# The first stage of a four-part network rewritten: heads as 32-row and 32-column tiles of the array, six unrolled slots, weights rounded by ACT

## The reference

```python
x = x + attn_a(layernorm(x), Wq, Wk, Wv, Wo, norm_w)      # this case's stage
x = x + ffn(layernorm(x), Wqkv, ..., W2, b2)              # 6 layers
x = x + attn_b(layernorm(x), W_Q, W_K, W_V)
x = x + ffn(layernorm(x), Wqkv, ..., W2, b2)              # the same 6 layers again

def attn_a(h):                                            # 8 heads of 16, chunks of 64
    q, k, v = h @ Wq.T, h @ Wk.T, h @ Wv.T
    o = causal linear attention: state (sum of k v^T of earlier chunks) times q,
        plus (q k^T * lower triangle) v inside the chunk
    z = cumsum(k, over tokens)
    o = o / max(|sum_over_the_head(q * z)|, 1)
    o = o * rsqrt(mean_over_the_head(o * o) + 1e-5) * norm_w
    return o @ Wo.T
```

## Time and profile before

| | |
|---|---|
| median of 3 runs | 3269.31 us (3267.53 to 3271.12) |
| the profiled execution's own time | 3269.6 us |
| its span, first to last instruction | 3267.8 us |
| mean granted clock of TensorE | 0.976 of 2.4 GHz |
| PE / DVE / ACT / POOL busy | 94% / 90% / 69% / 56% of the span |

### The profile page before, as it was taken

One profiled execution on the slowest core, in us unless ns is written; L12 is line 12 of the kernel. 1 busy time (PEld: TensorE's weight loads), 2 busy tenths in 40 slices (PEclk: granted clock), 3 DMA queues, 4 the chain that ended last, 5 costly groups with the idle time before them and its releaser, 6 DMA issues.

```text
span 3267.8 us, 93879 instructions
## 1 busy us (share of the span) xinstructions
PE 3067.1 (94%) x37848; PEld 1899.2 (58%) x37848; DVE 2927.5 (90%) x2712; ACT 2266.0 (69%) x3691; POOL 1814.5 (56%) x822
## 2 busy tenths in 40 slices
PE   5768999999999999999999999999999999999997
PEld 3535665565565565566566655665665655655663
DVE  4549999999999999999999999999999999999995
ACT  1136777777777777777666777777777777777774
POOL 5525555555555555555454555655655655656651
PEclk8778999999999999999999999999999999999998
DMA  5534454454454454455344445445445445445442
GB/s 174 185 99 113 105 147 118 105 147 118 104 146 119 104 145 121 103 144 141 87 120 107 104 105 145 121 103 145 120 103 146 119 105 146 117 106 146 115 117 57
DMA packets 254252, 398.01 MB, mean 122 GB/s; under 512 B 51132, under 2 KB 84984, under 8 KB 254136
## 3 DMA queue, kind: packets, MB, share of 16 engines
q1 hardware_dynamic: 254136, 396.48, 46.4%
HBM read 64.71 MB, written 19.92 MB: 26 GB/s over the span
## 4 chain that ended last, share of the span: by engine, by line
PE 39%; DVE 23%; ACT 19%; issue 9%; POOL 1%; SPq 1%; DMA 1%; DVEq 0%; ACTq 0%; POOLq 0%
PE ps L783 6%; PE ps L741 5%; PE ps L801 5%; PE ps L817 5%; PE ps L762 5%; PE ps L722 4%; DVE f_mx L1297 4%; ACT f_ab L1029 3%; DVE f_p L1300 3%; ACT f_u L1028 3%; DVE f_p L1312 3%; ACT ps L1040 3%; PE ps L724 3%; PE ps L723 3%; ACT f_p L1046 3%
## 5 line engine op out<-in xcount | busy, mean ns | idle before, releaser
L1226 POOL TENSOR_TENSOR f_w<-f_w,f_ab 128x1024 f32<-128x1024 f32 x192 | 549.0, 2859 | 527.3 <-DVE f_w L1277 527.3
L1231 POOL TENSOR_TENSOR f_ab<-f_w,f_rn 128x1024 f32<-128x1024 f32 x192 | 594.3, 3095 | 390.9 <-DVE f_rn L1287 374.1
L1222 POOL TENSOR_TENSOR f_u<-f_u 128x512 f32<-128x512 f32 x384 | 588.6, 1548 | 363.3 <-ACT f_u L1028 363.2
L1029 ACT ACTIVATE f_ab<-ps,f_pa 128x512 f32<-128x512 f32 x768 | 542.0, 706 | 1.2
L1028 ACT ACTIVATE f_u<-ps 128x512 f32<-128x512 f32 x768 | 467.0, 608 | 96.7 <-PE ps L724 91.5
L1277 DVE TENSOR_TENSOR f_w<-f_ab,f_tan 128x1024 f32<-128x1024 f32 x384 | 500.9, 1345 | 4.3 <-POOL f_ab L1231 2.3
L783 PEld LDWEIGHTS ps<-f_tb,f_v 128*64 128x64 f32 x6144 | 396.4, 138 | 102.7 <-issue 86.5
L783 PE MATMUL ps<-f_tb,f_v 128*64 128x160 f32 (+1 forms) x6144 | 442.7, 297 | 12.2 <-DMA f_tb<-f_pt 9.9
L1040 ACT ACTIVATE ps<-ps 128x512 f32<-128x512 f32 x384 | 204.7, 574 | 340.4 <-PE ps L741 340.1
L722 PE MATMUL ps<-f_xh,f_wh 128*128 128x512 f32 x768 | 380.7, 496 | 53.2 <-ACT f_ab L1029 43.7
L741 PE MATMUL ps<-f_u,f_ones 128*128 128x512 f32 x768 | 368.8, 601 | 6.1 <-POOL f_u L1222 5.1
(11 more groups left out here) (170 smaller groups left out, 4975.6 us busy)
## 6 DMA issues: line engine op xcount, KB each, us to landing
f_kb<-f_ab SPq DMA_DIRECT2D x384, 256.0 KB, 3.6
f_qb<-f_ab SPq DMA_DIRECT2D x384, 256.0 KB, 3.6
f_tb<-f_pt SPq DMA_DIRECT2D x1344, 64.0 KB
f_wh<-split_w SPq DMA_DIRECT2D x48, 384.0 KB, 4.4
f_wl<-split_w SPq DMA_DIRECT2D x48, 384.0 KB, 4.2
a_w_raw<-wqkv SPq DMA_DIRECT2D x24, 384.0 KB, 4.1
split_w<-a_w_hi SPq DMA_DIRECT2D x24, 384.0 KB, 2.3
split_w<-a_w_lo SPq DMA_DIRECT2D x24, 384.0 KB, 2.8
```

What stands on the lines that cost most here:

```text
L1029: nc.scalar.activation(ab[:, g % 2, i, :], bank("qk", g, i), ACT.Identity, scale=pa[:, g, i:i + 1]).then_inc(qk_read.sem, 1)
L1222: nc.gpsimd.tensor_tensor(u[:, 2 * i + 1, :], u[:, 2 * i, :], u[:, 2 * i + 1, :], ALU.add).then_inc(sq_sum[i].sem, 1)
L1226: nc.gpsimd.tensor_tensor(w[:, 0:2, :], w[:, 0:2, :], ab[:, k % 2, 0:2, :], ALU.add).then_inc(q_sum.sem, 1)
L1231: nc.gpsimd.tensor_tensor(ab[:, k % 2, 0:2, :], w[:, 0:2, :], rn[:, 0:1, :].broadcast_to([128, 2, N]), ALU.mult).then_inc(rope_q.sem, 1)
```

## The change

The function is the same, the data flow of `stage_a` is new, and `stage_ffn` is as it was.

- Heads are taken in pairs of one 32-row strip. q is copied twice (even and odd heads of each strip, `qm`), k once, v twice into arrays with zeros at the other parity (`vz`), all by ACT. Scores: for each tile of tokens four products of 32 rows and 256 columns, one for each strip of rows, into four banks (`tile_position=(32 * p, 0)`). Values: for each tile eight products of 128 rows, 32 columns of weights and 128 tokens (`tile_position=(0, 32 * p)`), so that the result comes out with the feature on the partition, and no transpose is left. DVE masks 2048 columns at a time, twice a batch.
- The division by the denominator and the norm are one expression: `o * (ss + 1e-5 * max(d, 1)^2)^-0.5`, by sums over the head as a product with `blockmask`.
- Six slots written out instead of a loop; slot k holds the front f of batch k, the middle s of batch k-1 and the end e of batch k-2, interleaved on each engine.
- The weight halves: ACT makes the rounded one, four copies of 128 x 768 a slot between its own operations (`round_weights`), POOL subtracts; four buffers; SP loads quad n+4 ahead of the stores of quad n.
- Loads: PE waits for x of its batch and the mean matrix only, ACT and later PE for 8 tables; x comes in four pieces, each with its semaphore.

The core of the new code (waits left out where they name only the operation before; functions of one instruction left out where the text says what they do):

```diff
+                SLOTS = [tuple(b if 0 <= b < B else None for b in (k, k - 1, k - 2)) for k in range(B + 2)]
...
+                    sp.dma_start(xT[:, cols(0)], x_rows[:, cols(0)]).then_inc(x_in[0], 16)
+                    sp.dma_start(mean_w[:, :], tabs["mean_w"]).then_inc(x_in[0], 16)
+                    for dst, src in ((wq, wa["wq"]), (wk, wa["wk"]), (wv_wk, wa["wv_wk"]), (parity, tabs["parity"]), (causal, tabs["causal"]),
+                                     (blockmask, tabs["blockmask"]), (wo, wa["wo"]), (nw, wa["nw"])):
+                        sp.dma_start(dst[:, :], src).then_inc(tables, 16)
...
+                    for n in range(QUAD_W):
+                        sp.wait_ge(lo_done, n + 1)
+                        if n + NW < QUAD_W:
+                            load_raw(n + NW)
+                        for part, w in enumerate((w_hi, w_lo)):
+                            sp.dma_start(split_w[n, part], w[:, n % NW].bitcast(F32)).then_inc(split_out[n % NW], 16)
...
+                    for n in range(QUAD_W):
+                        if n >= NW:
+                            pool.wait_ge(split_out[n % NW], 32 * (n // NW))
+                        pool.wait_ge(hi_done, n + 1)
+                        nc.gpsimd.tensor_tensor(w_lo[:, n % NW], w_raw[:, n % NW], w_hi[:, n % NW].bitcast(F32), ALU.subtract).then_inc(lo_done, 1)
...
+                    def scores(b, part):
...
+                        for i in (2 * part, 2 * part + 1):
+                            for p in range(4):
+                                rows = slice(32 * p, 32 * p + 32)
+                                last = nc.tensor.matmul(ps[:, p, 256 * (i % 2):256 * (i % 2) + 256], ks[rows, tile(i)], qm[rows, :, tile(i)], start=True, stop=True,
+                                                        tile_position=(32 * p, 0))
...
+                    def values(b, part):
...
+                        for i in (2 * part, 2 * part + 1):
+                            if i:
+                                for a in range(2):
+                                    nc.tensor.matmul(ps[:, O, tile(i)], state[:, i - 1, :], qm[:, a, tile(i)], start=a == 0, stop=False, skip_group_check=True)
+                            for a in range(2):
+                                for p in range(4):
+                                    rows = slice(32 * p, 32 * p + 32)
+                                    last = nc.tensor.matmul(ps[rows, O, tile(i)], vz[:, i, a, rows], st[:, part, p, 2 * (i % 2) + a, :], start=i == 0 and a == 0, stop=a == 1,
+                                                            skip_group_check=True, tile_position=(0, 32 * p))
...
+                    def round_weights():
+                        n = next(quads)
+                        act.wait_ge(raw_in[n % NW], 16 * (n // NW + 1))
+                        if n >= NW:
+                            act.wait_ge(split_out[n % NW], 32 * (n // NW))
+                        nc.scalar.activation(w_hi[:, n % NW], w_raw[:, n % NW], ACT.Copy).then_inc(hi_done, 1)
```

More of the change, by code:

```diff
@@ L114, in _, with tile @@
+                def tile(i):
+                    return slice(128 * i, 128 * i + 128)
+                SLOTS = [tuple(b if 0 <= b < B else None for b in (k, k - 1, k - 2)) for k in range(B + 2)]
                 @block.sync
                 def _(sp):
[L116 to L133, removed]
@@ L137, in _ @@
+                    for j in range(NW):
+                        sp.wait_ge(split_out[j], 32 * (QUAD_W // NW))
                 @block.gpsimd
                 def _(pool):
[L139 to L149, removed]
+                    nc.gpsimd.memset(vz[:, :, :, :], 0.0).then_inc(cleared, 1)
@@ new lines, in mean2, with variance2 @@
+                    def mean2(b):
+                        pe.wait_ge(A["x1"], b + 1)
+                        nc.tensor.matmul(ps[:, Y, :], mean_w[:, :], xT[:, cols(b)], start=True, stop=True).then_inc(A["mean2"], 1)
+                    def variance2(b):
+                        pe.wait_ge(A["sq2"], b + 1)
+                        nc.tensor.matmul(ps[:, Y, :], mean_w[:, :], sq2[:, :], start=True, stop=True).then_inc(A["var2"], 1)
+                    for f, s, e in SLOTS:
+                        if f is not None:
+                            mean(f)
+                        if s is not None:
+                            scores(s, 0)
+                        if e is not None:
+                            project_out(e)
+                        if s is not None:
+                            states(s)
+                        if f is not None:
+                            variance(f)
+                        if s is not None:
+                            scores(s, 1)
+                            values(s, 0)
+                        if e is not None:
+                            mean2(e)
+                        if s is not None:
+                            denominator(s)
+                            values(s, 1)
+                        if e is not None:
+                            variance2(e)
+                        if f is not None:
+                            project(f)
+                        if s is not None:
+                            squares(s)
@@ L278, in _, with square, deviation @@
-                    act.preload_act_table_set("natural_log_exp_and_others")
-                    act.wait_ge(loaded, 16 * LOADS)
-                    steps_of(act, step)
+                    def square(b):
+                        act.wait_ge(A["xc"], b + 1)
+                        nc.scalar.activation(sq[:, :], xc[:, :], ACT.Square).then_inc(A["sq"], 1)
+                    def deviation(b):
+                        act.wait_ge(A["var"], b + 1)
+                        nc.scalar.activation(sq[:, :], ps[:, M, :], ACT.Ln, bias=EPS).then_inc(A["lnv"], 1)
+                        act.wait_ge(A["lnv"], b + 1)
+                        nc.scalar.activation(ps[:, M, :], sq[:, :], ACT.Exp, scale=-0.5).then_inc(A["rstd"], 1)
@@ new lines, in _ @@
+                    act.wait_ge(tables, 16 * N_TABLES)
+                    for f, s, e in SLOTS:
+                        if f is not None:
+                            square(f)
+                            deviation(f)
+                        round_weights()
+                        if e is not None:
+                            square2(e)
+                        if s is not None:
+                            denominator(s)
+                        round_weights()
+                        if e is not None:
+                            deviation2(e)
+                        if s is not None:
+                            squares(s)
+                        round_weights()
+                        if f is not None:
+                            keys_and_queries(f)
+                            values(f)
+                            values_by_parity(f)
+                        round_weights()
+                        if s is not None:
+                            norm(s)
```

390 lines of the change are left out of this document (179 added, 211 removed).

## The result

| | before | after |
|---|---|---|
| median | 3266.46 us (6 runs, 3261.76 to 3271.12) | 3282.02 us (6 runs, 3279.39 to 3292.10) |
| ratio | | 1.0054 [1.0042, 1.0066] |
| first stage, to the first load of `zT` | 207.59 us | 116.60 us |
| the rest of the span | 3060.21 us | 3164.10 us |

The account below looks back on a forecast made before the run. The prediction took the first stage as a chain with PE in most links, no engine full; slots at two thirds high clock plus the tail end it at 132 instead of 206.3 us, gain 74.3, total 3195, range 3177 to 3230.

Parts of the forecast that it names:

- the 206.25 us: The changed first stage's length before, out of 3267.8 us; forecast to end at 132, a gain of 74.3.
- The tripwire on a second stage changed by more than 5 us: Sign of a wrong forecast: the second stage, expected to last 3061.5 us as before, changing by over 5 us.
- The start: First slot: the last table lands at 7.4 us, so ACT starts its square then instead of at 11.69.
- two thirds high: PE's clock in a full slot: high two thirds of the time, giving 25 us a slot.
- rival 1: First stage: PE's clock high throughout, stage 114 us, gain 92, total 3177; chance 17%.
- the tail of 7.3: End of the first stage: quads 22 and 23 behind deviation2 make it end 17.8 us after `scale` instead of 10.5.
- rival 3: First stage: weight loads set the pace, stage 170 us, gain 36, total 3233; chance 6%.
- the contention that I costed at nothing: DVE in a full slot: contention over SBUF costed at nothing, with a bound of 1 us a slot.
- the sum: PE's work in a full slot with four tiles at once: 16.0 us high clock, scores and values 1.7 each.
- rival 5: Score products: strips load weights one after another, 8 us more, 3203; inside the forecast's 55%.
- rival 4: Score and value tiles don't overlap: 3296 with the clock low, 3213 with it high; chance 3%.
- the way in and out of a group: Change of tiling on PE: 0.18 us an excursion, six of them 1.1 us a slot.

Follow-up runs that it names:

- 109: The kernel before with 109 more PE instructions (waits already met) at the end of PE's first-stage list: 3322.77 us.
- 125: The kernel before with 125 more PE instructions (waits already met) in the first stage: 3384.26 us.
- 141: The kernel before with 141 more PE instructions (waits already met) in the first stage: 3276.43 us.
- 200: The changed kernel with 200 more PE instructions (waits already met) at the end of PE's first-stage list: 3189.91 us.
- 236: The changed kernel with 236 more PE instructions (waits already met) at the end of PE's first-stage list: 3224.03 us.
- 100: The changed kernel with 100 more PE instructions (waits already met) at the end of PE's first-stage list: 3214.62 us.
- quads_ahead: The changed kernel with 40 added PE instructions and ACT's 24 weight roundings placed earlier, none in the last slot: 3169.26 us, ratio 0.9698 to the kernel before.
- pool_rounds: The changed kernel with 40 added PE instructions, POOL making the rounded weight half again and ACT none: 3162.21 us, ratio 0.968 to the kernel before.
- the 40: 40 more PE instructions (waits already met) ending PE's first-stage list; alone on the changed kernel: 3174.17 us, ratio 0.9713 to the kernel before.

## Why the prediction was wrong

**The step that failed**: "The second stage is untouched, so the forecast is the change of the 206.25 us." Its text was untouched; its place in instruction memory was not. The first loop moved from seven blocks to eight and lost 5.3 us in each of 20 steps, 106 us, which is the 103.9 of the windows to 2. At a turn in the timeline 3.76 us are standstill, and the seven products from 1115.37 to 1118.45 take 3.08 us where 0.23 from product to product at the high clock makes 1.6: 5.2 together. Over 19 turns the standstill is 4.05 a turn; that the low clock makes up the rest is argued, no run took it away alone. Without the fetches the same change takes 3174. No rival named this, though the queue's 71 packets, as many as one pass through the code, stood on the page. That the total came out within 0.5% of the kernel before is chance: a gain of 91 us and a loss of 104 with nothing to do with each other. The tripwire on a second stage changed by more than 5 us was the right one.

**The first stage**, step by step. The start was right (7.4 forecast, 7.36). Scores of batch 0 at 19.66 (21.7). Slot 1 took 16.2 us, the full slots 20.5 and 19.95, where I had 16.5 and 20.3 at the high clock: the links were right, and the mis-sized term is the clock, two thirds high where it was 1.00 to the end of the second full slot (76.25). I took 21 and 25, so rival 1 was this stage's case; it forecast 3177, and the loop with no fetches measures 3174. The slot without a front took 21.0 (21.5) at 0.79. From `scale` to `zT` 10.5 as before, and the tail of 7.3 behind it was 7.8, with 1.0 to the first load. By engine, the costliest groups of the kernel after (busy us, mean ns | idle before):

```profile
L145 POOL TENSOR_TENSOR a_w_lo<-a_w_raw,a_w_hi 128x768 fp32r<-128x768 f32 x24 | 43.2, 1810 | 66.5 <-ACT a_w_hi L326 66.4
L326 ACT ACTIVATE a_w_hi<-a_w_raw 128x768 fp32r<-128x768 f32 x24 | 19.8, 842 | 0.0
L374 DVE TENSOR_TENSOR a_st<-ps,a_causal 128x2048 f32<-128x2048 f32 x8 | 18.3, 2285 | 2.2 <-PE ps L183 2.2
L365 DVE TENSOR_TENSOR_SCAN a_ksum<-a_ks 128x512 f32<-128x512 f32 x4 | 8.9, 2223 | 11.8 <-ACT a_ks L277 11.8
```

A quad on ACT (0.84 forecast), a mask of 2048 (2.3), and POOL waiting for ACT and never for a load (rival 3 fell) are as predicted. The scan, 1331 ns in the earlier trace rows, is 2223: the contention that I costed at nothing hit its bound of 1 us a slot. The trace points at POOL's subtraction: the scans beside 0.77 and 1.43 us of it took 1.85 and 2.52 us, and one of the kernel before that only POOL's adding overlapped (24.09, for 1.04 us) took 1.22. No run took the subtraction away.

**The tiles.** 16 score instructions take 1.15 us, 0.072 each, between the 0.053 of the sum and the 0.116 of rival 5, and far from 0.213 with no overlap (rival 4). Inside such a group the fours start 0.216 us apart (in the group at 56.30 at 56.62, 56.84 and 57.06), 0.054 an instruction: the pace is that of the sum, and the rest of the 1.15, 0.3 us, is the way in and out of a group, for which I had 0.18. It is alike for the values: inside a group the fours start 0.109 apart, the 0.027 of the sum, and 16 take 0.65 us.

```profile
88.53 0.65 PE L209 MATMUL ps<-a_st,a_vz 128*32 128x128 f32 x16
```

Rival 5's pace is that of `weigh` at the high clock in the kernel before:

```profile
46.21 1.86 PE L178 MATMUL ps<-a_vk,a_st 128*128 128x16 f32 x16
```

The Trainium skill's rule that a weight load takes time by its columns (TensorE: Matmul & The Clock Gate, LDWEIGHTS) would have given 0.116 had strips loaded one after another; the trace shows that the loads of different strips overlap.

**The fetch.** The Trainium skill (Runtime: NRT & Kernel Launch, Instruction fetch mechanics) gives PE room for 2048 instructions, refilled in blocks of 256, and calls crossing a block mostly hidden. The runs agree on the blocks (71 packets for 18,371 instructions) and on the crossing: the last straight steps, 44 to 46, fetch 6 or 7 blocks each and take 61.1 to 61.7 us, a step of the loop 61.4. On the room they agree only in part: 2048 instructions are eight blocks, but a loop over seven stays and one over eight is fetched again, except where only its last 12 to 19 instructions lie in the eighth. It also says that a taken branch out of a window of two blocks forces a fetch; here the measurement decides otherwise, since a loop over seven blocks turns with none. By the room alone the 1612 instructions fit wherever they start, and by the branch rule both kernels would fetch at every turn; only the count of blocks together with the room, which I didn't make, puts this loop close enough to the edge to be a rival.

## What to carry to other kernels

A hardware loop near the capacity of an engine's instruction memory is tied to the length of the code ahead of it: count its body in blocks before lengthening anything upstream, and where the count can tip, pad by a few instructions. Before believing that an untouched stage became slower, look at the instruction queue's packets: more than one pass through the code means refetching, and the steps that hold them say where. Work moved onto an engine whose instructions are links of the chain can lengthen the chain, even where that engine idles for 40% of the time (ACT was busy 12.1 of 20 us in a slot): look at what it stands between, and give it out where the engine waits.

## What the runs showed that I had not expected

- A turn over eight blocks costs 1.9 to 5.3 us with the same nine fetches; what differs is how many instructions lie before the first edge.
- A wait already met costs PE 0.054 us, 0.108 for the two of one instruction: between PE's last product of the stage and the first load of `zT` lie 11.20, 12.92 and 14.65 us with 109, 125 and 141 instructions, and 21.30 and 25.17 with 200 and 236. In the changed kernel up to 100 cost nothing, because PE has 10.9 us there while ACT and POOL finish; with `quads_ahead` and `pool_rounds` the 40 reach past the end by some 0.6 us (an estimate: 2.65 and 2.69 us from the start of the last `zT` to the first load, 2.03 in the kernel before).
- What lies ahead of my count differs between the two kernels by 9 to 28 instructions. Whether that is the runtime's code or a fault of the count stays open, so a pad is found by trying, not by counting alone.
